# One wait fewer ahead of VectorE's normalisation in the first of three stages

## The chip, the core and the metric

The kernel runs on one core of one Trainium2 chip. The metric is the device time of an execution in microseconds (us). Engines are called TensorE (PE in the profile, its weight loads PEld), VectorE (DVE), ScalarE (ACT), GpSimd (POOL) and SyncE (SP), which issues most of the DMAs.

## The reference

For a batch of B = 2048 samples of N = 50 nodes with D = 32 features and T = 2 maskers:

```python
fusion = x.reshape(b, n * d)
adj = jnp.einsum('bn,tnm->btm', fusion, masker_param) + masker_bias
adj = jax.nn.relu(adj).reshape(b, t, n, n)
adj = adj / (adj.sum(axis=-1, keepdims=True) + 1e-06)
h = jnp.broadcast_to(x[:, None], (b, t, n, d))
m = jnp.einsum('btnd,de->btne', h, weight[0])
m = jnp.einsum('btnm,btmd->btnd', adj, m)
gates = m @ w_ih.T + b_ih + h @ w_hh.T + b_hh
r, z, ng = jnp.split(gates, 3, axis=-1)
h = (1.0 - sigmoid(z)) * tanh(sigmoid(r) * ng) + sigmoid(z) * h
```

Then follow a normalisation over the batch, one over each sample, a softmax over the nodes and a weighted sum. Everything is in 32-bit floats. The relu and the division by the row sum in the first lines are where the change lies.

## The kernel before

The kernel has three stages, one after the other, each a block of five instruction streams, one per engine.

**First stage.** It computes `adj`. The batch is 16 tiles of 128 samples, in 2 blocks of 8 (BLK). The 5000 columns of the masker matrices are 10 groups of 500 columns (ten rows of 50). One *product* is one tile times one group: 38 matmuls with 500 columns each into one bank of PSUM, each of the 13 slices of the contraction taken in up to three parts (high times low, low times high, high times high). There are 20 iterations (2 blocks x 10 groups) of 8 products, 160 in all. In each block the first and the last iteration are written out for ScalarE and VectorE, and the eight between are a hardware loop (`p1_iters`, L449 to L455) whose body holds one iteration.

After product c, ScalarE's `relu` (L298 to L302) moves the bank into `u[:, c % 2]`. VectorE's `normalise` (L337 to L349) sums the rows of `u` into `rows` (L340), adds the small constant (L342), takes the reciprocal (L344) and multiplies `u` with it into `an` (L348). `turn_squares` (L351 to L358) transposes `an` in squares of 32 x 32 into `at[:, c % 2]` and counts up `at_ready`; SyncE's `store_tile` (L197) stores `at` in HBM as `adjT`. There is one buffer `an`, and it is read by the transpose of product c - 1 and written by the multiply of product c. Both are VectorE's, in this order. VectorE also makes the low halves of x and of the weights (L264 to L267, L289, L293) in the same stream.

The waits in `normalise` are on `dve_step`, which VectorE itself counts up after each small step, and, ahead of the multiply, on `at_ready` reaching c, that is, on the transpose of product c - 1.

**Second stage.** It goes over the 16 tiles, two a pass. A pass has 16 steps, 8 for each of its tiles. Passes 0 and 7 are written out and passes 1 to 6 are a hardware loop on every one of ScalarE (L631), VectorE (L709) and TensorE (L803):

```python
m_halves(0, 0)
turn(0, True)
with dve.Fori(1, TILES // 2 - 1) as it:
    turn(it, True)
turn(TILES // 2 - 1, False)
```

In each step TensorE multiplies x with `adj` (L746) and computes the gates (L773, L779); ScalarE splits off the high part `m_hi` (L579) and applies the sigmoids (L609, L614) and the tanh (L619); VectorE makes the low part `m_lo` (L644), which TensorE's gates wait for, `n_in` (L654), and the new h (L664 to L669). The last VectorE instruction of a pass is the transpose of a part of h (L688), the first of the next pass is `m_lo`. ScalarE issues the load of the next tile's x, `xg` (`reload_xg`, L563), in the first step of each half pass, and splits it into `xg_hi` from the fifth step of that half on (L575). SyncE loads `adj_sb` and `xs_sb` for the tile after next when a tile's products are done (L532 to L538). ScalarE stores the results as `hF`.

**Third stage.** It computes the normalisations, the softmax and the weighted sum, all written out.

Of the kernel before, what the change touches and what calls it, by code (L numbers as in the profile page):

```python
# [145 lines left out]
def stage1(nc, place, psum, ins, adjT, shared):  # L146
    xT, W = ins["xT"], ins["W"]
    with ExitStack() as ctx:  # L148
# [20 lines left out]
        an_cleared, at_ready = sem("an_cleared"), sem("at_ready")  # L169
# [90 lines left out]
        def split_x_lo(dve, bt, half):  # L260
            dve.wait_ge(x_hi_ready, 2 * bt + half + 1)
            w = bt % BLK
            k0, k1 = (0, XH) if half == 0 else (XH, KF)
            last = nc.vector.tensor_tensor(x_lo[:, w, k0:k1, :], x_raw[:, k0:k1, :], x_hi[:, w, k0:k1, :].bitcast(fp32),  # L264
                                           ALU.subtract)
            if half:
                last = nc.vector.tensor_tensor(x_lo[KR:P, w, KF, :], x_raw[KR:P, KF, :], x_lo[KR:P, w, KF, :].bitcast(fp32),  # L267
                                               ALU.subtract)
            last.then_inc(x_ready, 1)
# [15 lines left out]
        def split_w_lo(dve, i, it):  # L285
            dve.wait_ge(w_hi_ready, it * NU + i + 1)
            k0, k1 = UNITS[i]
            if i < NU - 1:
                nc.vector.tensor_tensor(w_lo[:, k0:k1, :], w_raw[:, k0:k1, :],  # L289
                                        w_hi[:, k0:k1, :].bitcast(fp32), ALU.subtract).then_inc(w_ready, 1)  # L290
            else:

                nc.vector.tensor_tensor(w_lo[0:BIAS_HI, KF, :], w_raw[0:BIAS_HI, KC, :],  # L293
                                        w_lo[0:BIAS_HI, KF, :].bitcast(fp32), ALU.subtract).then_inc(w_ready, 1)
# [39 lines left out]

        @block.vector
        def _(dve):
            def normalise(c, c2, first=False):  # L337

                dve.wait_ge(u_ready, c + 1)
                nc.vector.tensor_reduce(rows[:, 0], u[:, c2], AX.X, ALU.add).then_inc(dve_step, 1)  # L340
                dve.wait_ge(dve_step, 3 * c + 1)
                nc.vector.tensor_scalar_add(rows[:, 1], rows[:, 0], EPS_ROW).then_inc(dve_step, 1)  # L342
                dve.wait_ge(dve_step, 3 * c + 2)
                nc.vector.reciprocal(rows[:, 2], rows[:, 1]).then_inc(dve_step, 1)  # L344
                dve.wait_ge(dve_step, 3 * c + 3)
                if not first:
                    dve.wait_ge(at_ready, c)
                nc.vector.tensor_tensor(an[:, :, 0:N], u[:, c2], rows[:, 2].unsqueeze(2).to_broadcast([P, GN, N]),  # L348
                                        ALU.mult).then_inc(an_ready, 1)  # L349

            def turn_squares(c, c2, start=False):  # L351

                dve.wait_ge(an_ready, c + 1)
                if start:
                    dve.wait_ge(an_cleared, 1)
                else:
                    dve.wait_ge(at_stored[c2], 8 * (c - c2))
                nc.vector.transpose(at[:, c2], an[:].rearrange("p n (k s) -> p k n s", s=TB)).then_inc(at_ready, 1)  # L358

            def weight_blocks(dve):  # L360

                wd = shared.wd
                dve.wait_ge(w_ready, ITERS * NU)
                nc.vector.memset(wd[:], 0.0).then_inc(zeroed, 1)
                dve.wait_ge(zeroed, 1)
                dve.wait_ge(shared.weights_loaded, 64)
                dve.wait_ge(g_product, 1)
                for j in range(4):
                    q = slice(D * j, D * j + D)
                    pair, one = divmod(j, 2)  # L370
                    at = {R_G: SH * pair + D * one, Z_G: SH - SH * pair + D * one, N_G: D * j}
                    for gate, first in at.items():
                        of, e = (N_W if gate == N_G else RZ_W), slice(D * gate, D * gate + D)
                        nc.vector.tensor_copy(wd[q, 0, of, first:first + D], g_bank[q, e])
                        last = nc.vector.tensor_copy(wd[q, 1, of, first:first + D], shared.whh4[q, e])
                last.then_inc(blocks_ready, 1)
                nc.vector.tensor_tensor(shared.bias[:], shared.biases[:, 0], shared.biases[:, 1], ALU.add).then_inc(shared.bias_ready, 1)

            nc.vector.memset(an[:, :, N:MPAD], 0.0).then_inc(an_cleared, 1)
            split_x_lo(dve, 0, 0)  # L380
            for i in range(NU):
                split_w_lo(dve, i, 0)
                if i == 0:
                    split_x_lo(dve, 0, 1)
            for blk in range(BLOCKS):
                for it, group in p1_iters(dve, blk):
                    static = isinstance(it, int)
                    for w in range(BLK):
                        c = it * BLK + w
                        if not (static and it == 0 and w == 0):  # L390
                            normalise(c - 1, (w - 1) % 2, first=static and it == 0 and w == 1)
                            turn_squares(c - 1, (w - 1) % 2, start=static and it == 0 and w <= 2)
                        if static and it == GROUPS and w == 0:
                            for half in range(2):
                                split_x_lo(dve, 2 * BLK - 1, half)
                        if static and it == 0 and w + 1 < BLK:
                            for half in range(2):
                                split_x_lo(dve, w + 1, half)
                        if w == BLK - 1 and not (static and it == ITERS - 1):
                            for i in range(NU):  # L400
                                split_w_lo(dve, i, it + 1)
                        if static and it == GROUPS - 1 and w >= 1:
                            for half in range(2):
                                split_x_lo(dve, BLK + w - 1, half)
                        if static and it == ITERS - 1 and w == 2:
                            weight_blocks(dve)
                        if static and it == ITERS - 1 and w == 4:
                            dve.wait_ge(wd_hi_ready, 1)
                            nc.vector.tensor_tensor(shared.wd_lo[:], shared.wd[:], shared.wd_hi[:].bitcast(fp32),
                                                    ALU.subtract).then_inc(shared.wd_ready, 1)  # L410
            normalise(ITERS * BLK - 1, 1)
            turn_squares(ITERS * BLK - 1, 1)

# [35 lines left out]
def p1_iters(eng, blk):  # L449

    base = blk * GROUPS
    yield base, 0
    with eng.Fori(1, GROUPS - 1) as g:
        yield base + g, g
    yield base + GROUPS - 1, GROUPS - 1  # L455
# [1017 lines left out]
```

## Time and profile before

| what | us |
|---|---|
| median of 3 runs | 2257.29 |
| lowest and highest run | 2251.59, 2257.75 |
| the profiled execution | 2254.87 |
| its span, first to last instruction | 2253.1 |
| TensorE busy | 2141.4 (95%) |
| VectorE busy | 1221.3 (54%) |
| ScalarE busy | 866.1 (38%) |

The span is that of the program's own instructions; 1.8 us of the execution lie around it. Part 2 of the page cuts the span in 40 slices and shows the busy share in tenths (9 is 90% or more):

```profile
PE   8999999999999999999999999998988988996898
DVE  5444334444265443344443453776776766878667
```

The first stage is the first 24 to 25 slices, with TensorE full throughout; the second is the next 12 and the third the rest.

### The profile page before, as it was taken

Reading aid. Unit: us, or ns where it says so; the run is one execution under the profiler, and the core shown is the slowest. Engines: PE = TensorE matmul, PEld = TensorE weight load, DVE = VectorE, ACT = ScalarE, POOL = GpSimd, SP = SyncE. Lnnn points to the kernel's source line nnn. Section 1 sums busy time; section 2 is a strip of 40 time slices with the busy share of each in tenths; the row PEclk is TensorE's granted clock in tenths of the full one; section 3 lists DMA queues with packets and bytes.
Section 4 is the critical chain, followed back from the end, with each engine's and each line's share of the span. In section 5 each row is a group of like instructions: output and inputs, shape, how many; then the busy total and the mean of one; then the engine's idle time right before and its main releaser. Section 6 shows DMA issues by size and latency. Waiting matters only on the chain. (4 is left out here: it accounts for less than half of the span.)

```text
span 2253.1 us, 33249 instructions
## 1 busy us (share of the span) xinstructions
PE 2141.4 (95%) x11694; PEld 1680.5 (75%) x11694; DVE 1221.3 (54%) x2370; ACT 866.1 (38%) x1471; POOL 66.7 (3%) x68
## 2 busy tenths in 40 slices
PE   8999999999999999999999999998988988996898
PEld 7888888888888888888888887776766766775333
DVE  5444334444265443344443453776776766878667
ACT  4211111111033111111110123776876776875862
POOL 0000000000000000000000000100100110110000
PEclk9999999999999999999999999998999998998899
DMA  7321222221254212222202234675556566564660
GB/s 249 140 100 51 93 99 104 99 95 45 104 187 147 105 56 83 99 104 102 101 35 104 104 103 119 160 171 162 150 153 167 137 158 171 141 177 138 196 184 11
DMA packets 148058, 276.08 MB, mean 123 GB/s; under 512 B 11565, under 2 KB 106061, under 8 KB 143053
## 3 DMA queue, kind: packets, MB, share of 16 engines
q1 hardware_dynamic: 129836, 237.53, 34.7%
q10 hardware_dynamic: 18144, 37.69, 5.6%
q8 instruction: 28, 0.46, 0.1%
q14 instruction: 50, 0.40, 0.1%
HBM read 196.01 MB, written 79.17 MB: 122 GB/s over the span
## 5 line engine op out<-in xcount | busy, mean ns | idle before, releaser
L431 PE MATMUL psum<-w_hi,x_lo 128*128 128x500 f32 x2080 | 806.3, 388 | 8.2 <-DVE w_lo L289 8.2
L431 PE MATMUL psum<-w_lo,x_hi 128*128 128x500 f32 (+1 forms) x2080 | 807.8, 388 | 0.0
L431 PE MATMUL psum<-w_hi,x_hi 128*128 128x500 f32 x1920 | 743.2, 387 | 0.0
L340 DVE TENSOR_REDUCE rows<-u 128x10 f32<-128x500 f32 x160 | 107.7, 673 | 741.4 <-ACT u L302 741.3
L302 ACT ACTIVATE u<-psum 128x500 f32<-128x500 f32 x160 | 93.9, 587 | 1048.0 <-PE psum L431 1048.0
L431 PEld LDWEIGHTS psum<-w_hi,x_lo 128*128 128x128 f32 x2080 | 391.0, 188 | 88.8 <-issue 8.2
L431 PEld LDWEIGHTS psum<-w_lo,x_hi 128*128 128x128 f32 (+1 forms) x2080 | 390.8, 188 | 78.1
L431 PEld LDWEIGHTS psum<-w_hi,x_hi 128*128 128x128 f32 x1920 | 360.6, 188 | 72.3
L746 PE MATMUL psum<-adj_sb,xs_sb 100*64 100x100 f32 x2048 | 222.6, 375 | 4.4 <-PEq L148 4.4
L746 PEld LDWEIGHTS psum<-adj_sb,xs_sb 100*64 100x64 f32 x2048 | 154.7, 153 | 55.8 <-issue 39.4
L609 ACT ACTIVATE r_gate<-psum,bias 64x400 f32<-64x400 f32 x256 | 151.2, 591 | 60.5 <-PE psum L773 58.9
L283 ACT CAST w_hi<-w_raw 128x1000 fp32r<-128x1000 f32 (+1 forms) x140 | 136.1, 972 | 46.4 <-PE psum L431 45.1
L358 DVE STREAM_TRANSPOSE at<-an 128x640 f32<-128x640 f32 x160 | 135.3, 846 | 13.3
L614 ACT ACTIVATE psum<-psum,bias 64x400 f32<-64x400 f32 x256 | 141.1, 551 | 2.3 <-DVE hG L669 0.5
L289 DVE TENSOR_TENSOR w_lo<-w_raw,w_hi 128x1000 fp32r<-128x1000 f32 x120 | 137.7, 1190 | 3.7 <-ACT w_hi L283 2.2
L726 POOL TENSOR_TENSOR xg_lo<-xg_sb,xg_hi 128x400 fp32r<-128x400 f32 x64 | 66.5, 1041 | 1956.5 <-ACT xg_hi L575 1956.5
L773 PE MATMUL psum<-m_hi,wd_lo 64*128 64x400 f32 x256 | 60.4, 467 | 64.4 <-DVE m_lo L644 36.8
L654 DVE SCALAR_TENSOR_TENSOR n_in<-psum,bias,r_gate 128x400 f32<-128x400 f32 x128 | 80.1, 626 | 76.0 <-PE psum L779 44.3
L348 DVE TENSOR_TENSOR an<-u,rows 128x500 f32<-128x500 f32 x160 | 108.9, 681 | 5.4
L677 DVE BATCH_NORM_STATS2 stats<-hC 128x128 f32 (+1 forms) x400 | 88.1, 281 | 43.2 <-ACT hC L587 40.6
L773 PEld LDWEIGHTS psum<-m_hi,wd_lo 64*128 64x128 f32 x256 | 25.2, 191 | 108.0 <-issue 66.6
L644 DVE TENSOR_TENSOR m_lo<-psum,m_hi 128x400 fp32r<-128x400 f32 x128 | 70.7, 553 | 43.3 <-issue 38.8
(168 smaller groups left out, 2103.9 us busy)
## 6 DMA issues: line engine op xcount, KB each, us to landing
w_raw<-W SPq DMA_DIRECT2D x140, 500.0 KB, 6.5
adjT<-at SPq DMA_DIRECT2D x160, 320.0 KB, 2.3
adj_sb<-adjT SPq DMA_DIRECT2D x32, 800.0 KB
xs_sb<-xz SPq DMA_DIRECT2D x16, 1600.0 KB
hF<-hC ACTq DMA_DIRECT2D x96, 256.0 KB, 2.9
h<-hF SPq DMA_DIRECT2D x64, 256.0 KB, 4.0
adj_sb<-adjT SPq DMA_DIRECT2D x32, 450.0 KB
xg_sb<-xg ACTq DMA_DIRECT2D x14, 800.0 KB, 17.3
```

What stands on the lines that cost most here:

```text
L283: nc.scalar.copy(w_hi[:, k0:k1, :], w_raw[:, k0:k1, :]).then_inc(w_hi_ready, 1)
L289: nc.vector.tensor_tensor(w_lo[:, k0:k1, :], w_raw[:, k0:k1, :], w_hi[:, k0:k1, :].bitcast(fp32), ALU.subtract).then_inc(w_ready, 1)
L302: nc.scalar.activation(u[:, c2].rearrange("p n m -> p (n m)"), mm_out(c2), ACT.Relu).then_inc(u_ready, 1)
L340: nc.vector.tensor_reduce(rows[:, 0], u[:, c2], AX.X, ALU.add).then_inc(dve_step, 1)
L348: nc.vector.tensor_tensor(an[:, :, 0:N], u[:, c2], rows[:, 2].unsqueeze(2).to_broadcast([P, GN, N]), ALU.mult).then_inc(an_ready, 1)
L358: nc.vector.transpose(at[:, c2], an[:].rearrange("p n (k s) -> p k n s", s=TB)).then_inc(at_ready, 1)
L431: last = nc.tensor.matmul(mm_out(w % 2), a[0:r, w, k, :], b[0:r, k, :], start=k == 0 and n == 0, stop=k == KF and n == 1)
L609: last = nc.scalar.activation(r_gate[half], rz_bank(pair)[half], ACT.Sigmoid, bias=bias[half, R_G:R_G + 1])
L614: last = nc.scalar.activation(z_bank[half], rz_bank(pair)[other], ACT.Sigmoid, bias=bias[other, Z_G:Z_G + 1])
L677: last = nc.vector.bn_stats(stats[:, bass.ds(tile, 1), c, :].rearrange("p i v -> p (i v)"), hC[:, c, :])
L746: last = nc.tensor.matmul(out_[SH * i:SH * i + SH, :, gi], xs[r][:, b, :], adj[r][:, i, :, q * QB + gi], start=True, stop=True)
L773: last = nc.tensor.matmul(rz_bank(pair), w[half], m[half], start=first, stop=final)
```

## The change

`normalise` no longer waits on `at_ready`; its parameter `first`, which left that wait out for the first product, goes with it. `at_ready` is still counted up, for SyncE. Nothing else is touched.

```diff
-            def normalise(c, c2, first=False):
+            def normalise(c, c2):
...
                 dve.wait_ge(dve_step, 3 * c + 3)
-                if not first:
-                    dve.wait_ge(at_ready, c)
                 nc.vector.tensor_tensor(an[:, :, 0:N], u[:, c2], rows[:, 2].unsqueeze(2).to_broadcast([P, GN, N]),
                                         ALU.mult).then_inc(an_ready, 1)
...
                         if not (static and it == 0 and w == 0):
-                            normalise(c - 1, (w - 1) % 2, first=static and it == 0 and w == 1)
+                            normalise(c - 1, (w - 1) % 2)
```

An instruction carries one wait of its own. The multiply carries that on `dve_step`; the one on `at_ready` was an instruction by itself in VectorE's stream, ahead of the multiply.

## Rows read from the trace of the kernel before

**Rows 1.** Stretches: microseconds, busy time (instructions) of each engine, clock, DMA share, GB/s

```profile
8.22:1382.35 1374.13, 1374.13 (x6082) 1142.36 (x6082) 592.52 (x1008) 264.34 (x379) 0.00 (x0) 1.00 0.29 103
1382.35:1386.72 4.37, 0.00 (x0) 0.03 (x1) 2.59 (x5) 0.77 (x2) 0.00 (x0) 1.00 0.01 5
```

**Rows 2.** Groups of instructions, VectorE, 0 to 1386 us: busy, mean ns, idle before

```profile
L348 DVE TENSOR_TENSOR an<-u,rows 128x500 f32<-128x500 f32 x160 | 108.9, 681 | 5.4
L340 DVE TENSOR_REDUCE rows<-u 128x10 f32<-128x500 f32 x160 | 107.7, 673 | 741.4 <-ACT u L302 741.3
L344 DVE RECIPROCAL rows<-rows 128x10 f32<-128x10 f32 x160 | 34.7, 217 | 5.5
```

**Rows 3.** Waits, 1386.7 to 2074 us: total us, times, longest

```profile
PE psum L773 <- DVE m_lo L644: 36.8, 6, 7.5
DVE m_lo L644 <- issue: 38.8, 5, 8.1
```

**Rows 4.** Timeline at a pass's start: start, us, instruction, idle before it

```profile
1647.86 0.57 DVE L644 TENSOR_TENSOR m_lo<-psum,m_hi 128x400 fp32r<-128x400 f32 x1 [7.69 <-issue]
1648.48 0.70 PE L773 MATMUL psum<-m_hi,wd_lo 64*128 64x400 f32 x2 [7.10 <-DVE m_lo L644]
```

**Rows 5.** DMA queues, 1639.2 to 1647.8 us, then 1553 to 1638.6: packets, MB, share

```profile
q14 instruction: 2, 0.02, 0.6%
...
q14 instruction: 5, 0.04, 0.2%
```

**Rows 6.** Timeline, VectorE, the first stage's last product

```profile
1384.17 0.68 DVE L348 TENSOR_TENSOR an<-u,rows 128x500 f32<-128x500 f32 x1
```

**Rows 7.** DMA queues, 148.5 to 149.5 us, then 2218 to 2220

```profile
q14 instruction: 1, 0.01, 3.3%
...
q14 instruction: 1, 0.01, 1.1%
```

**Rows 8.** The page's part 3, DMA queues over the span: packets, MB, share

```profile
q14 instruction: 50, 0.40, 0.1%
```

**Rows 9.** DMA queues, 707 to 708 us, then 2196 to 2197.5

```profile
q14 instruction: 1, 0.01, 1.9%
...
q14 instruction: 1, 0.01, 1.3%
```

**Rows 10.** Timeline, ScalarE, its first instruction after its jump at 1637.3

```profile
1637.67 0.49 ACT L579 CAST m_hi<-psum 128x400 fp32r<-128x400 f32 x1 [0.46 <-PE psum L746]
```

**Rows 11.** Waits, 1985 to 2012 us, first half of the last pass

```profile
ACT xg_hi L575 <- DMA xg_sb<-xg: 5.5, 1, 5.5
DVE n_in L654 <- ACT r_gate L609: 5.3, 1, 5.3
```

**Rows 12.** Timeline, VectorE, L654 of steps around four pass starts

```profile
1464.81 0.63 DVE L654 SCALAR_TENSOR_TENSOR n_in<-psum,bias,r_gate 128x400 f32<-128x400 f32 x1
...
1513.58 0.61 DVE L654 SCALAR_TENSOR_TENSOR n_in<-psum,bias,r_gate 128x400 f32<-128x400 f32 x1
...
1549.42 0.63 DVE L654 SCALAR_TENSOR_TENSOR n_in<-psum,bias,r_gate 128x400 f32<-128x400 f32 x1
...
1600.97 0.61 DVE L654 SCALAR_TENSOR_TENSOR n_in<-psum,bias,r_gate 128x400 f32<-128x400 f32 x1
...
1895.01 0.63 DVE L654 SCALAR_TENSOR_TENSOR n_in<-psum,bias,r_gate 128x400 f32<-128x400 f32 x1
...
1946.05 0.61 DVE L654 SCALAR_TENSOR_TENSOR n_in<-psum,bias,r_gate 128x400 f32<-128x400 f32 x1
...
1980.78 0.63 DVE L654 SCALAR_TENSOR_TENSOR n_in<-psum,bias,r_gate 128x400 f32<-128x400 f32 x1
...
2028.90 0.62 DVE L654 SCALAR_TENSOR_TENSOR n_in<-psum,bias,r_gate 128x400 f32<-128x400 f32 x1
```

**Rows 13.** Timeline, VectorE, fifth step of a pass's second half

```profile
1620.83 0.63 DVE L654 SCALAR_TENSOR_TENSOR n_in<-psum,bias,r_gate 128x400 f32<-128x400 f32 x1 [2.83 <-ACT r_gate L609]
```

**Rows 14.** Instructions of tile xg_sb: its loads, issue to landing

```profile
DMA to landing us min/median/max: 4.9/15.1/20.2
```

## The prediction

> **What bounds the kernel now.** I read the page's parts 1 and 2 first, then the stretches, then the waits. The stretches of the profiled span are to be seen first [rows 1]: from the first matmul on come 1374.13 us in which TensorE is busy for all 1374.13 us (first stage), then a gap of 4.37 us with no matmul; the rest, 866 us, is stages two and three. In the first stage VectorE, on which the edit lies, works 592 of 1374 us. So the first stage ends when TensorE's stream ends, and VectorE's 741 us of idle time ahead of its reductions, waiting for ScalarE's relu [rows 2], cost nothing. The gap of 4.37 us is the one place where the last product's normalisation is on the path.
>
> In the second stage the longest wait of TensorE is on VectorE: 36.8 us in 6 waits for m_lo, and VectorE itself was late there for no data but for "issue", 38.8 us in exactly 5 waits [rows 3]. One of them [rows 4]: VectorE ends a transpose, the last instruction of a pass of its loop (L709), and starts the next pass's m_lo 7.69 us later; TensorE has waited 7.10 us for it. The loop has six passes, so five jumps back, and each has this stall. Between the two, two packets of an instruction queue (q14) come in, and five from one jump to the next [rows 5]. I read it as an instruction fetch: the jump's target was no longer at hand.
>
> **The change, part by part.** *The wait.* It disappears in 159 executed products (one of 160 had none). Price: ahead of the reciprocal, which stands behind one wait, VectorE idles 5.5 us over 160, that is 0.034 us each; ahead of the multiply, behind two waits, 5.4 us, also 0.034 [rows 2]. The second wait adds nothing between the two instructions: it is met by then. So 159 x 0.00 = 0, with bounds of -0.03 and +0.03 us a product: at most 5 us of VectorE's time, all under TensorE's matmuls, since 741 us of slack stand there. Without that cover (the last product, whose multiply is at 1384.17 [rows 6], in the gap) it is at most 0.03 us once. The order of transpose and next multiply is kept by their engine. No DMA moves and no wait is added. Directly, the edit is worth 0.
>
> *The places of the instructions behind it.* This is the part that I take for larger. VectorE's program gets shorter. The wait stands 47 times in it: 6 in the first iteration written out, 8 in each of two loop bodies, 8 in each of three more iterations written out, 1 at the end. Everything of VectorE behind them, the second stage's loop too, moves 47 places forward. I counted places in VectorE's recorded stream, register, wait and branch instructions included (4443 executed, loops counted once). The first-stage loops end at places 193 and 448, the second-stage loop is 688 to 976 (289 instructions). Six fetch packets, the first at 148.97 us and the last at 2218.93, came when VectorE stood at places 192, 316, 448, 1218, 1343 and 1469 [rows 7]. Modulo 128 these are 64, 60, 64, 66, 63, 61: its program comes in blocks of 128 that begin near 64 + 128k, one fetched at each crossing. The packets show sizes that fit (50 of 0.40 MB, 8 KB each) [rows 8]. So the loop now touches four blocks (from 576, 704, 832, 960); at its end the fourth was entered and a fifth called for. Moved by 47 it is 641 to 929 and touches three (576, 704, 832). Do three stay at hand? ScalarE's loop is the test: places 442 to 685 of its stream, three of its packets, from 707.18 to 2196.61 us, at 194, 963 and 1089 (66, 67, 65 modulo 128) [rows 9], hence blocks from 320, 448 and 576; and behind its jump back it idles 0.46 us, for TensorE [rows 10]. Three stay, so I expect all five stalls of VectorE to go. The weak point: 442 is only 6 places from an edge; were the edge there, ScalarE's loop would speak for two blocks only.
>
> A rule of the Trainium skill speaks against this (page "Runtime: NRT & Kernel Launch", section "Instruction fetch mechanics"): instruction memory is two lines of 16 KiB, and a taken branch whose target isn't in the current two pages waits for a fetch. By it a loop of 289 instructions ahead of a third, prefetched page would go on stalling, and the time would stay. The packets of 8 KB and ScalarE's free jump [rows 8, 10] don't fit lines of 16 KiB.
>
> *What is late next.* Not all of the stall is won. The step behind each jump issues ScalarE's load of xg, needed four steps later. Passes without a stall ahead of them show what comes: in the last one ScalarE waits 5.5 us for xg and VectorE 5.3 us behind it [rows 11], where the pass from 1648 has no such wait. The stall gave that load time, since SyncE's large loads, begun some 13 us before, drain meanwhile. I therefore price whole stretches, from the gate step (L654) ahead of the jump to that of step 8 behind it [rows 12]. With the stall there are five; the first is 1549.42 to 1600.97 = 51.55, the last 1895.01 to 1946.05 = 51.04 us, and they sum to 255.6. Without: 1464.81 to 1513.58 = 48.77 and 1980.78 to 2028.90 = 48.12 us. The second has the same loads in flight, the first also early loads of constants, so I take the second: 5 x 48.12 = 240.6, 15.0 us less; by the first 243.9, 11.7 less. I take the middle, 13.4. Bounds: a half pass for the other tile (from 1600.97) waits 2.83 us for the same cause where this one waits 5.3 [rows 13]; with that 2.5 us more a jump would be won, 12.5, so about 26 in all; and were xg never late, the whole 38.8 us of the five waits.
>
> **Rivals.** *The stall stays.* Fewer than three blocks stay at hand, and ScalarE's loop touches two only, because its edge is at 442 and not at 448. Then VectorE's moved loop still misses its first block at each jump, only the wait goes, worth 0, and the time is 2257 (2251 to 2260 by the runs' spread). The rule of the Trainium skill named above gives the same outcome. For it: the 6 places of margin. Against: the free jump. *The gain is larger.* xg is hardly late in the new passes: 2257.3 less 28 to 38.8, 2218 to 2229. Against it: both passes that have no stall ahead show the wait. *Slower: the load of xg lands later still.* With VectorE's stall gone the tile loads, the stores of hF and xg are closer together; the longest landing of xg now is 20.2 us [rows 14]. The forecast wins 2.7 us a jump, so it turns into a loss once xg lands over 22.9 us behind its issue; at 25 us it is 5 x 2.1 = 10 us slower, 2268. Against it: the last full pass issued the same loads 13 us ahead and landed at about 20. *The change doesn't do what it says:* a race would show in results, not in time; nothing here would reorder VectorE.
>
> **The numbers.** The sum is 2254.87 (the profiled execution, span 2253.1) - 13.4 = 2241.5; that execution is 2.4 us under the median of 2257.29, so on medians 2243.9; I say 2244. Chances: stalls gone, xg late 0.69 (2229 to 2250); stalls gone, xg not late 0.04; stall stays 0.22; slower by the xg load 0.05. The likeliest case's own range is 2229 to 2250. Nearly a quarter lies with the time of before, so the range reaches there: 2228 to 2259. A measurement of this kernel can tell about 0.3%, 6.8 us, from no change. Faster by more: 0.69 + 0.04 less 0.02 for a gain under 6.8 us = 0.71. Within: 0.22 + 0.02 = 0.24. Slower: 0.05.
>
> **What would show it.** In the changed kernel's trace: 159 instructions fewer in all (33090); idle time ahead of the multiply still 0.034 us; TensorE busy through the first stage, its last matmul within 1 us of 1382. The waits of the second stage: "m_lo for issue" gone, and TensorE's for m_lo down from 36.8 to a few us. Instead ScalarE waits some 5 us for xg in the first half of every pass, as in the last one now [rows 11]. From one jump to the next no packets in queue q14, where five are now. Wrong would be: the five waits of 7.5 to 8 us still there (the blocks), or gone with no gain (the stretches), or a first stage whose length changed.

## The result, and the profile after

The changed kernel takes 2234.31 us (median of 4 runs, 2231.27 to 2236.71), beside 2257.16 (4 runs, 2251.59 to 2257.75) for the kernel before on the same chip: a ratio of 0.9911, 95% interval 0.9894 to 0.9927, 22.9 us less. The forecast was 2244, in a range of 2228 to 2259; the likeliest case's own range, 2229 to 2250, holds the result too. The profiled execution took 2232.1 us.

From the page of the changed kernel: the span and the number of instructions, the busy times, TensorE's busy tenths, and the instruction queue q14, which carries the blocks of VectorE and of ScalarE.

```profile
span 2230.3 us, 33090 instructions
PE 2134.4 (96%) x11694; PEld 1676.3 (75%) x11694; DVE 1220.1 (55%) x2370; ACT 865.1 (39%) x1471; POOL 66.7 (3%) x68
PE   8999999999999999999999999999999999896898
q14 instruction: 24, 0.20, 0.0%
```

There are 159 instructions fewer, as worked out. VectorE is busy for the same time as before, 1220 us, and q14 carries 24 packets where it carried 50 [rows 8]. None of them falls into the loop's passes 2 to 6: between 1534 and 1975 us the trace has no packet of q14. In the slices of the second stage TensorE is at 9 throughout, where single slices of the kernel before stood at 8.

Groups of instructions of VectorE in the first stage, with the idle time before them behind the last bar, answer [rows 2]:

```profile
L346 DVE TENSOR_TENSOR an<-u,rows 128x500 f32<-128x500 f32 x160 | 108.9, 681 | 5.4
L340 DVE TENSOR_REDUCE rows<-u 128x10 f32<-128x500 f32 x160 | 107.7, 673 | 742.1 <-ACT u L302 742.0
L344 DVE RECIPROCAL rows<-rows 128x10 f32<-128x10 f32 x160 | 34.7, 217 | 5.5
```

The multiply, from which the wait was taken, still has 5.4 us of idle time ahead of 160 executions. The wait that the change removes was worth nothing where it stood. TensorE's last product of the stage and the last normalisation, from the timeline (start, duration):

```profile
1384.64 0.39 PE L429 MATMUL psum<-w_lo,x_hi 97*128 97x500 f32 x1
1386.85 0.68 DVE L346 TENSOR_TENSOR an<-u,rows 128x500 f32<-128x500 f32 x1
```

Both are 2.7 us later than before [rows 1, 6]. All of it arises in the first 16.4 us, while the first weights come in (timeline, TensorE):

```profile
11.64 0.78 PE L429 MATMUL psum<-w_hi,x_lo 128*128 128x500 f32 x1 [0.92 <-DVE w_lo L289]
...
16.37 0.39 PE L429 MATMUL psum<-w_hi,x_hi 128*128 128x500 f32 x1
```

There is one wait of 0.92 us for the low half of the weights that the execution before didn't have, and the matmuls start 0.42 us apart up to 16.37 us and 0.23 us apart from there on, where before they did so from 11.6 us. It seems to go with the execution and not with the kernel: of five kernels below that are alike up to the last iteration of this stage (the changed one with 24, 28, 48, 32 and 40 instructions more), three reach the second stage's first gate step at 1396.6, 1396.8 and 1397.0 us and two at 1394.0 and 1394.1, one profiled execution each. What sets the slower pace of the first matmuls stays open; the profile gives the granted clock as 1.00 in both stretches. From 20 us on the stage runs as before.

Waits of the second stage (1386.7 to 2050 us): engine, line, waited for, total us, times, longest. They answer [rows 3].

```profile
ACT xg_hi L573 <- DMA xg_sb<-xg: 57.9, 13, 6.2
DVE n_in L652 <- ACT r_gate L607: 53.3, 13, 5.6
...
PE psum L771 <- DVE m_lo L642: 1.0, 1, 1.0
```

VectorE's 38.8 us of "m_lo for issue" are gone, and with them TensorE's wait for m_lo, from 36.8 to 1.0 us. In their place ScalarE waits 57.9 us in 13 waits for the load of xg; before, the same wait was 34.0 us in 8. At a jump back of the loop (timeline, VectorE) the transpose is followed at once by the next pass's m_lo, where there were 7.69 us of idle time [rows 4]:

```profile
1719.82 1.01 DVE L686 STREAM_TRANSPOSE hT<-hG 128x800 f32<-128x800 f32 x1
1720.76 0.54 DVE L642 TENSOR_TENSOR m_lo<-psum,m_hi 128x400 fp32r<-128x400 f32 x1
```

**Where the 22.8 us of span are.** Over stretches cut as in the prediction (from the gate step ahead of a jump to step 8 behind it), the first and the last of the five, each with its two ends, answer [rows 12]; the rows are starts of L652. The first is 47.3 us long, beside 51.55 before, the last 43.8, beside 51.04.

```profile
1553.76 0.63 DVE L652 SCALAR_TENSOR_TENSOR n_in<-psum,bias,r_gate 128x400 f32<-128x400 f32 x1
1601.04 0.61 DVE L652 SCALAR_TENSOR_TENSOR n_in<-psum,bias,r_gate 128x400 f32<-128x400 f32 x1
...
1879.11 0.63 DVE L652 SCALAR_TENSOR_TENSOR n_in<-psum,bias,r_gate 128x400 f32<-128x400 f32 x1
1922.91 0.61 DVE L652 SCALAR_TENSOR_TENSOR n_in<-psum,bias,r_gate 128x400 f32<-128x400 f32 x1
```

| part of the span | before | after | difference |
|---|---|---|---|
| start up to the second stage's first gate step | 1393.64 | 1396.32 | +2.7 |
| pass 0, first half | 39.58 | 41.23 | +1.7 |
| pass 1, first half | 48.77 | 48.81 | 0.0 |
| the five first halves behind a jump back | 255.5 | 226.1 | -29.4 |
| last pass, first half | 48.12 | 47.06 | -1.1 |
| all eight second halves | 274.1 | 279.1 | +5.0 |
| from the last gate step to the end | 193.35 | 191.72 | -1.6 |

The gain stands where the stalls were. It is larger than the predicted 13.4 us, and 5 us of it are given back in the second halves of the passes.

### The profile page after: what moved, and what is told of

It reads as the page before. It is cut to its first block and busy times, and to the rows that moved or that the text cites. A ratio compares the mean times of both kernels' runs of the same rounds, so it can differ in the third digit from the quotient of the medians.

```text
span 2230.3 us, 33090 instructions
## 1 busy us (share of the span) xinstructions
PE 2134.4 (96%) x11694; PEld 1676.3 (75%) x11694; DVE 1220.1 (55%) x2370; ACT 865.1 (39%) x1471; POOL 66.7 (3%) x68
## 5 line engine op out<-in xcount | busy, mean ns | idle before, releaser
L283 ACT CAST w_hi<-w_raw 128x1000 fp32r<-128x1000 f32 (+1 forms) x140 | 136.1, 972 | 46.7 <-PE psum L429 45.2
L652 DVE SCALAR_TENSOR_TENSOR n_in<-psum,bias,r_gate 128x400 f32<-128x400 f32 x128 | 79.9, 625 | 91.9 <-ACT r_gate L607 53.3
L1105 DVE SCALAR_TENSOR_TENSOR pr<-h,nmu_sb,psum 128x512 f32<-128x512 f32 x100 | 70.0, 742 | 27.8 <-PE psum L1286 26.6
```

The lines of the kernel that those rows point to most:

```text
L283: nc.scalar.copy(w_hi[:, k0:k1, :], w_raw[:, k0:k1, :]).then_inc(w_hi_ready, 1)
L1105: V.scalar_tensor_tensor(out=pr[:, g % PR_BUFS], in0=h_of(i, c), scalar=nmu[:, c:c + 1], in1=wb_bank(k), op0=ALU.add, op1=ALU.mult).then_i ...
```

## The experiments

**Are the stalls a matter of the wait or of places?** The first theory is the prediction's: VectorE's instructions come in blocks of 128, and the loop now touches three of them, not four. If so, dummy instructions that do nothing must bring the stalls back without the wait, and must take them away with the wait left in. In the changed kernel the loop lies at places 641 to 929. Each of these kernels adds waits that have long been met, in the last iteration of the first stage only, ahead of VectorE's second stage (two waits share one instruction, so NW is twice the number of instructions wanted; the value differs from kernel to kernel):

```diff
+                        if static and it == ITERS - 1:
+                            for _ in range(NW * (w + 1) // BLK - NW * w // BLK):
+                                dve.wait_ge(an_cleared, 1)
```

*48 instructions more in the changed kernel* (33138 recorded, loop at 689 to 977, the blocks from 576 to 960 again).

> The changed kernel, plus waits that are already met, put between the products of the first stage's last iteration on VectorE, where it idles some 6 us a product. They fill 48 places of its stream, so the second stage's loop stands at places 689 to 977, one from where it was before the change; the wait on at_ready stays away. Theory places (the loop touches a fourth block of 128, from 960, and its first is gone at each jump): the five waits of 7.5 to 8 us for issue come back and the time is that of before, 2257 (2252 to 2260). Theory wait (the gain is from VectorE's normalisation running without its wait): the gain stays, 2234 (2230 to 2238).

Measured: 2257.63 us (10 runs), ratio 1.0015 (0.9999 to 1.0031) to the kernel before, which takes 2254.43 on that chip. From its page and its waits:

```profile
span 2255.5 us, 33138 instructions
...
q14 instruction: 49, 0.40, 0.1%
```

```profile
DVE m_lo L645 <- issue: 38.4, 5, 8.0
```

The wait is still gone, and the time, the five stalls and the packets are those of the kernel before. The whole effect of the change is one of places.

*40 instructions more in the kernel before, its wait left in* (loop at 728 to 1016: three blocks, from 704, 832 and 960).

> The kernel before, its wait on at_ready kept, with 40 places MORE in front of the second stage's loop: 728 to 1016, which touches the blocks from 704, 832 and 960, three. Theory places: no stall although nothing was taken away, 2234 (2230 to 2238) and 40 instructions more than before. Theory wait: 2257 or a little slower for the added instructions. Theory of a shorter program: slower than 2257.

Measured: 2233.05 us (4 runs), ratio 0.9904 (0.9878 to 0.993), on the same chip. Page, then ScalarE's longest wait in the second stage:

```profile
span 2229.2 us, 33289 instructions
...
q14 instruction: 24, 0.20, 0.0%
```

```profile
ACT xg_hi L578 <- DMA xg_sb<-xg: 60.9, 14, 5.5
```

Forty dummy instructions make the kernel before as fast as the changed one; no wait of VectorE for issue is left, and the load of xg is waited for as in the changed kernel.

*24 and 40 instructions more in the changed kernel* (665 to 953, three blocks; 681 to 969, four blocks, the fourth entered by 10 instructions).

> As a_pad47 with 24 places: the loop stands at 665 to 953, 7 short of a block's edge at 960. Theory places: still three blocks (576, 704, 832), no stall, 2234 (2230 to 2238), no packets of queue q14 from one jump to the next. If what counts were only the number of instructions in the program, about half of the gain would be gone, 2245.

> As a_pad24 with 40 places: the loop stands at 681 to 969, 9 past the edge at 960. Theory places: a fourth block is entered, all five stalls are back, 2257 (2252 to 2260). A gradual theory would give a value between those of a_pad24 and a_pad47; an edge that lies further on, or that counts only when the block is well entered, would leave it at 2234.

Measured: 24 more give 2234.72 us, ratio 0.9907 (0.9877 to 0.9936), with 24 packets; 40 more give 2255.18 us, ratio 1.001 (0.9993 to 1.0027), with 49 packets and this wait:

```profile
DVE m_lo L645 <- issue: 37.1, 5, 7.8
```

*28 and 32 more*, one run each, to find the edge (669 to 957; 673 to 961).

> As a_pad24 with 28 places: the loop stands at 669 to 957. With the edge at 960 and no reading ahead: no stall, about 24 packets in queue q14, 2234. If the engine reads some places ahead of what it executes, the fourth block is called for and the stalls are there: about 49 packets, 2257.

> As a_pad24 with 32 places: the loop stands at 673 to 961. By an edge at 960 its last places lie in the fourth block, so: stalls, about 49 packets in queue q14, 2257. No stall if the edge is a few places further on.

Measured: 2239.95 us with 28 more, 2258.04 with 32 more. Page of the first, then page and wait of the second:

```profile
span 2238.2 us, 33118 instructions
...
q14 instruction: 24, 0.20, 0.0%
```

```profile
span 2256.3 us, 33122 instructions
...
q14 instruction: 50, 0.40, 0.1%
```

```profile
DVE m_lo L645 <- issue: 41.4, 5, 9.0
```

Four instructions of no effect cost 18 us. The single run with 28 more is 6 us over the 2234 that was expected, but it has no wait of VectorE for issue behind a jump. The edge is between a loop that ends at 957 and one that ends at 961, and the prediction had put it at 960 (64 + 128 x 7) from six fetch packets. A theory of growing distance, by which a longer way back costs more, falls with these two: the loop has 289 instructions in both.

**What takes part of the gain back?** The prediction said: the load of xg, issued in the pass's first step, lands late beside SyncE's large tile loads. In the changed kernel this is one load (timeline, ScalarE; the number in brackets is the idle time before, and what ended it):

```profile
1800.60 0.36 ACTq L143 DMA_DIRECT2D xg_sb<-xg  x1
...
1820.01 0.52 ACT L573 CAST xg_hi<-xg_sb 128x400 fp32r<-128x400 f32 x1 [4.97 <-DMA xg_sb<-xg]
```

The 800 KB are in use 19.4 us after the issue. SyncE had issued a tile's adj (two parts of 800 KB and two of 450) and xs (1600 KB), 4.1 MB in all, 13 to 11 us ahead of it, and their queue ran empty 17.1 us after xg's issue; xg is used 2.3 us behind that. In that load's time the two queues move this (DMA queues from 1800.6 to 1820 us: packets, MB, share; q1 is SyncE's, q10 ScalarE's):

```profile
q1 hardware_dynamic: 145, 1.96, 43.8%
q10 hardware_dynamic: 675, 1.66, 33.6%
```

So half of the 4.1 MB had been moved when xg was issued, and xg shares its own queue with ScalarE's stores of hF (256 KB each). It is the same for all loads of the loop's passes but the first, which is used 20.75 us after its issue: SyncE's drained 14.7 to 17.6 us after xg's issue, and xg was used 17.0 to 19.6 us after it, 2.0 to 2.5 us later. Two things could be meant by "beside": what is queued ahead, or what shares the DMA engines. Three kernels tell.

*xg first, in the same queue.* SyncE issues xs, then xg, then adj; ScalarE's load goes. The other kernel is the same edit on the kernel before.

```diff
                         sp.wait_ge(ax_done, (tile + 1) * ROUNDS)
-                        load_adj(sp, shared, adjT, tile + 2, r)
                         load_xs(sp, shared, ins, tile + 2, r)
+                        sp.wait_ge(h_ready, (tile + 1) * ROUNDS)
+                        load_xg(sp, shared, ins, tile + 2, r)
+                        load_adj(sp, shared, adjT, tile + 2, r)
...
-                    if q == 0 and (r and more or not r and not (isinstance(it, int) and it == 0)):
-                        reload_xg(it * 2 + r + 1, 1 - r)
```

> The changed kernel with the load of xg issued by SyncE, in the same queue as the tile loads: for each tile first xs, then, when the tile before it has left the slot, xg, and only then the four loads of adj. ScalarE issues no xg. In the changed kernel ScalarE waits 57.9 us for xg in 13 waits, which end about 2.3 us after the last tile load has drained. Theory that the tile loads ahead of it make xg late: these waits go nearly all, and the second stage shortens by 45 to 65 us, to about 2180 (2170 to 2195), if adj is still in time (needed in the seventh step of the half, some 26 us after). Rival, that xg is late by its own length or by ScalarE's late issue: the waits stay and the time stays at 2234. A second rival: adj becomes late instead, TensorE waits for adj_sb, and the time is 2215 to 2240.

> The same edit on the kernel before, whose five stalls of VectorE stay. If xg is what gave part of the gain back, then with xg out of the way the change is worth the whole stall: this run stands 5 x 7.8 to 5 x 9 = 39 to 45 us over a_xgfirst (the wait, and TensorE's slower matmuls behind it), against the 22.8 us between the kernels as they were. If it is again 23 us over, the lost part went elsewhere.

Measured on the changed kernel: 2167.22 us (4 runs, 2166.57 to 2169.62), ratio 0.9622 (0.96 to 0.9643) to the kernel before. It beats both kernels, and by more than was expected (2170 to 2195): the waits for xg go, and adj isn't late. The time from the issue of xg to its landing (shortest, median, longest), first in the changed kernel and then here, and ScalarE's longest wait of its second stage:

```profile
DMA to landing us min/median/max: 4.5/18.4/20.7
```

```profile
DMA to landing us min/median/max: 4.5/5.5/7.6
...
ACT r_gate L604 <- PE psum L766: 63.5, 128, 2.7
```

No wait for xg is left. Each first half of a pass of the loop takes 41.4 us and the five together 207.1, each second half of the loop 31.4: what ScalarE waits for is mostly TensorE, which now sets the pace. By this the late xg loads were worth 19.0 us in the changed kernel's five first halves (226.1 less 207.1) and 28.0 us in its eight second halves (279.1 less 251.1).

Measured on the kernel before with the same edit: 2205.82 us, ratio 0.9788 (0.9767 to 0.981). The two kernels differ by 38.6 us, and for VectorE in nothing but the places and a wait that was shown to cost nothing. So this is the price of the stalls when no late xg stands behind them, just under the 39 to 45 us that were expected. It comes about in another way than expected, though, and that it equals the 38.8 us of [rows 3], the prediction's farthest bound, is chance. The waits of VectorE in the second stage, and one jump in the timeline:

```profile
DVE m_lo L639 <- issue: 14.5, 5, 3.4
DVE n_in L649 <- issue: 9.0, 2, 4.6
```

```profile
1621.47 1.01 DVE L683 STREAM_TRANSPOSE hT<-hG 128x800 f32<-128x800 f32 x1
1625.87 0.57 DVE L639 TENSOR_TENSOR m_lo<-psum,m_hi 128x400 fp32r<-128x400 f32 x1 [3.38 <-issue]
...
1630.18 0.54 DVE L639 TENSOR_TENSOR m_lo<-psum,m_hi 128x400 fp32r<-128x400 f32 x1
1635.36 0.63 DVE L649 SCALAR_TENSOR_TENSOR n_in<-psum,bias,r_gate 128x400 f32<-128x400 f32 x1 [4.63 <-issue]
```

And the same step behind another jump:

```profile
1553.19 0.64 DVE L649 SCALAR_TENSOR_TENSOR n_in<-psum,bias,r_gate 128x400 f32<-128x400 f32 x1 [5.06 <-PE psum L774]
```

The idle time at the jump is 3.4 us here instead of 7.7. Of SyncE's loads only xs was in flight when VectorE began the pass's last transpose, where before adj and xs were; xg was issued at 1621.5 us and adj from 1622.0 to 1623.5, so partly within the idle time. But a second wait stands two steps on, with adj now in flight. It is there behind all five jumps, 3.5 to 5.1 us long and 21.5 us in sum. The profile puts two of them down to issue and three to TensorE, which ended 0.05 to 0.6 us before VectorE went on. The packets of q14 show that it is the same wait each time: VectorE's next instruction starts 1.6 to 1.7 us after the end of a packet, in all five. At the jumps themselves it does so 1.7 to 1.8 us after the second packet in the kernel before (1646.14 to 1647.86 at the jump of [rows 4]) and 1.35 to 1.7 us here. That ties the stalls to the fetch, packet by packet. The two waits come to 36.0 us (14.5 and 21.5). TensorE's clock falls between them. Stretches from the jump on: length, busy time of PE, PEld, DVE, ACT and POOL, granted clock, DMA share, GB/s:

```profile
1621.40:1626.50 5.10, 2.31 (x21) 1.51 (x20) 1.64 (x3) 1.59 (x3) 0.00 (x0) 0.90 0.87 246
1626.50:1632.00 5.50, 5.50 (x24) 4.55 (x26) 3.58 (x6) 3.77 (x7) 0.00 (x0) 0.50 1.02 204
```

After a wait in which TensorE was busy for 2.31 of 5.10 us the clock is granted at half, 1.2 GHz, for a stretch in which TensorE does nothing but work. The two gate steps around this jump take 8.5 and 9.0 us, beside 5.0 and 4.3 in the kernel without stalls.

*xs first and adj held back, xg left with ScalarE.* Here nothing but the order of SyncE's loads changes: xs, then the wait for `h_ready`, then adj. xg has less ahead of it and still shares the DMA engines.

> The changed kernel with the load of xg left with ScalarE; SyncE loads xs for the tile after next first and holds the four loads of adj back until the tile before has been finished, which is when ScalarE issues xg. Then no tile load is queued ahead of xg, but adj runs beside it. Theory that what is in flight ahead makes xg late: xg lands within 8 to 14 us of its issue in place of 17 to 19.5, before it is needed, the waits of ScalarE for xg (57.9 us in 13) go, and the time is that of a_xgfirst, 2160 to 2180. Rival: what counts is the total in flight beside it, adj as well: the waits stay at half or more, 2195 to 2235.

Measured: 2187.82 us (4 runs), ratio 0.9705 (0.9686 to 0.9724). Landing of xg, and ScalarE's wait for it:

```profile
DMA to landing us min/median/max: 4.5/16.7/17.2
...
ACT xg_hi L574 <- DMA xg_sb<-xg: 30.3, 12, 3.1
```

This lies between the two theories: the time is under the rival's range, but the landing is 1.7 us shorter in the median, not 10, and half of the waits is left, as the rival had it. In one load's time the two queues move this (1775.7 to 1792.6 us):

```profile
q1 hardware_dynamic: 225, 2.24, 56.8%
q10 hardware_dynamic: 497, 1.47, 30.3%
```

SyncE had issued only adj's 2.5 MB near xg's issue, where it had been 4.1 MB before it. But as adj was issued so late, more of it was still to come, 2.24 MB beside the 1.96 of the changed kernel, so the shorter landing isn't for fewer bytes. For the first 6 us after xg's issue no packet of ScalarE's queue moves at all. SyncE's queue ran empty 16.0 to 17.1 us after xg's issue in the loop's passes, and xg was used 16.3 to 17.2 us after it: again the two end together. So here the small load on another queue ends about when everything in flight beside it does, even where it is issued within 2.3 us of the large one; put ahead of adj in adj's own queue, at the same point of the pass, it lands in 5.5 us. That kernel changes two things, the place ahead of adj and the queue, which is no longer the one of the hF stores; which of them counts was not tested. Small as the gain in landing is, the kernel is 46 us faster (42 us, if each is held to the kernel before on its own chip, 2257.2 and 2253.0): the waits for xg fall from 57.9 to 30.3 us, the longest from 6.2 to 3.1, and the granted clock rises from 0.978 to 0.987 in the mean. How much is due to each wasn't measured.

## Why the prediction came out as it did

**The wait itself: right.** 5.4 us of idle time ahead of the multiply before and after; with 48 dummy instructions put in, the kernel has the time of before though the wait is gone.

**The first stage's end: missed by 2.7 us.** The last matmul was to be within 1 us of 1382 and is at 1384.64. The start did that, which varies between the profiled executions of kernels that are alike there; the prediction had taken it as fixed.

**The places: right**, to within four instructions, and so was the inference that three blocks stay at hand. The rule of the Trainium skill that was weighed against it (page "Runtime: NRT & Kernel Launch", section "Instruction fetch mechanics": two lines of 16 KiB, and a taken branch to a target outside them waits for a fetch) doesn't hold for VectorE here: packets are of 8 KB (24 carry 0.20 MB), and a loop of 289 instructions that lies in three such blocks fetches nothing between its jumps (no packet of q14 from 1534 to 1975 us). That a branch out of the blocks at hand waits is borne out, at 7.4 to 8.3 us a jump in these kernels (37.1 to 41.4 us over 5).

**What is late next: the mechanism right, its size off.** The prediction took the five new stretches as the middle of two passes that have no stall ahead, 48.77 and 48.12 us, and so 13.4 us less. They came out at 226.1 us for five, 45.2 each, 29.4 less. It wasn't this one execution: the five sum to 229.9, 228.2 and 229.6 us in the kernels with 24, with 40 in the kernel before, and with 28 more, and to 253.6, 251.1 and 258.4 in those with 48, 40 and 32 more. The means, with the two original kernels among them, are 228.5 and 254.7, 26.2 us apart. The step that failed is the choice of the sample. Passes 1 and 7 stayed where they were (48.81 and 47.06 us), but the five between are not like them: xg is used 17.0 to 19.5 us after its issue in these, and 20.7 and 20.1 us in passes 1 and 7. The prediction's "some 5 us" of waiting in every first half were 2.6 to 5.0 in these five. The term for the five stretches was thus put at 13.4 us and measured 26 to 29. The prediction had set 26 us as a bound, from the half pass with a wait of 2.83 us [rows 13], and that would have been the better value.

The clock makes a small difference of landing large. Two passes of the changed kernel, first the wait for xg and then the step behind it (columns as above):

```profile
1734.80:1740.80 6.00, 5.83 (x50) 4.33 (x46) 3.59 (x10) 3.30 (x8) 1.04 (x1) 1.00 0.51 192
1740.80:1745.40 4.60, 3.54 (x28) 2.99 (x30) 3.49 (x9) 4.34 (x9) 1.05 (x1) 1.00 0.15 57
```

```profile
1813.30:1821.70 8.40, 5.84 (x50) 4.34 (x46) 3.59 (x10) 3.29 (x8) 1.03 (x1) 1.00 0.48 168
1821.70:1828.30 6.60, 5.51 (x24) 4.60 (x26) 3.66 (x10) 5.71 (x11) 1.03 (x1) 0.52 0.10 40
```

In the first ScalarE waited 2.55 us for xg, and the next step takes 4.6 us at the full 2.4 GHz. In the second it waited 4.97 us, and the next step takes 6.5 us at 0.52, the lower level. So 2.4 us of waiting cost 4.3 us. The three of the five passes that had the shorter waits (gate steps of 7.3, 6.0 and 6.7 us) kept the clock; the two with 8.4 and 8.5 didn't, nor did passes 1 and 7 wholly (9.7 and 9.0).

**What was given back** hardly shows as a term: the second halves are 5.0 us longer in sum, but among the kernels without stalls they lie between 279.1 and 287.7 us, and among those with stalls between 274.1 and 283.4, so only the means (282.9 and 279.1) speak for some 4 us.

**The rivals.** "The stall stays" rested on the six places of margin; for VectorE they are real, since its edge lies between 957 and 961, a multiple of 128 from 448 within the same four places. ScalarE's loop was moved in no run by itself. "Slower" needed xg landings over 22.9 us; the longest is 20.7. "The gain is larger" took xg as hardly late; it was late, with 57.9 us of waits. That case was seen only with xg first, where the stalls' whole 38.6 us come out.

**Open.** Why xg lands later in passes 1 and 7 than in those between. In pass 1 SyncE's queue still moves loads of constants, until 24.1 us after xg's issue, but that they cause it was only argued; for pass 7 I have no reason. Whether the second wait in the kernel before with xg first is held up by the adj loads wasn't tested by itself, and neither was what the stores of hF in xg's own queue cost it.

## What to carry to other kernels

When an edit adds or removes an instruction ahead of a hardware loop, count where the loop then lies: an idle time put down to "issue" behind each jump back, with packets in the engine's instruction queue beside it, is a loop that touches one block too many, and a few dummy instructions, or a few less, settle it. Compare kernels only with their loops in the same blocks, or a change is credited with what its length did. And when a stall goes, look at what it gave time to: here a small load that is needed soon, beside large ones. Put ahead of them in their own queue it gave 67 us on the changed kernel (2234.3 to 2167.2; 62 us, if each is held to the kernel before on its own chip), nearly three times what the edit gave.

## What the runs showed of the hardware

- VectorE's instructions are fetched in blocks of 128 (8 KB). A loop of 289 runs free in three blocks and stalls at every jump back when it touches a fourth: 2239.95 us with its end at 957, 2258.04 at 961.
- VectorE's first instruction behind the jump starts 1.7 to 1.8 us after the second packet's end, at all five jumps of the kernel before (1646.14 to 1647.86).
- The fetch at a jump isn't of fixed cost: VectorE idled 7.4 to 8.3 us for it in the mean with adj and xs in flight. It was 2.9 us (14.5 over 5) with xs in flight and xg and adj just being issued, but then a second wait of 3.5 to 5.1 us followed two steps on.
- A load of 800 KB on ScalarE's queue, which the hF stores use too, took 18.4 us in the median. In the loop it was used 2.0 to 2.5 us behind the end of the 4.1 MB that another queue had begun 13 us earlier (1.96 MB of them moved after its issue, in the load that is shown); ahead of adj in the large loads' queue it took 5.5 us.
- Behind a wait of 2.55 us for xg TensorE's granted clock stayed at 1.00; behind one of 4.97 us a step ran at 0.52.
